# Cross-attention block with MLP: where GpSimd adds the MLP's output bias, and 28 warming matmuls

## The reference

```
q = layer_norm(x) @ q_w + q_b;  k = ctx @ k_w + k_b;  v = ctx @ v_w + v_b     # 16 heads of 32
p = softmax(q k^T / sqrt(32));  hidden = (p v) @ cproj_w + cproj_b + x
y = gelu(layer_norm(hidden) @ fc_w + fc_b)                                     # 512 -> 2048
out = hidden + (y @ proj_w + proj_b)                                           # 2048 -> 512
```

## Time and profile before

| | us |
|---|---|
| median of 3 runs | 719.77 |
| lowest, highest | 718.78, 721.11 |
| profiled execution, whole | 721.0 |
| its span, first to last instruction | 719.2 |

### The profile page before, as it was taken

How to read it: one execution, slowest core, us unless ns; L and a number is a source line. 1 busy time by engine, 2 the same in 40 slices (tenths; PEclk the granted TensorE clock), 3 DMA queues, 4 the chain that set the end, 5 groups by cost and what they waited for, 6 DMA issues and landing times.

```text
span 719.2 us, 13448 instructions
## 1 busy us (share of the span) xinstructions
PE 689.6 (96%) x4685; PEld 599.0 (83%) x4685; DVE 439.7 (61%) x867; ACT 313.8 (44%) x591; POOL 256.8 (36%) x228
## 2 busy tenths in 40 slices
PE   6889999999999999998899999999999999999998
PEld 5679898999998998897787888888888888888886
DVE  5689979979798888679865584423234322341122
ACT  4467867867676877578511023121111111111110
POOL 5285866657475758557503021011100111000000
PEclk9999999999999999999999999999999999999999
DMA  8895564637464644446109000100001000010001
GB/s 249 242 228 169 179 179 153 199 114 206 120 190 133 193 129 132 144 118 191 32 19 289 0 1 1 58 1 2 0 1 58 0 0 0 0 59 0 1 1 58
DMA packets 51153, 69.25 MB, mean 96 GB/s; under 512 B 8344, under 2 KB 29208, under 8 KB 51104
## 3 DMA queue, kind: packets, MB, share of 16 engines
q1 hardware_dynamic: 50832, 68.07, 32.3%
q0 software_dynamic: 272, 0.54, 0.4%
HBM read 47.21 MB, written 20.99 MB: 95 GB/s over the span
## 4 chain that ended last, share of the span: by engine, by line
PE 81%; DVE 5%; issue 4%; DMA 3%; ACT 3%; POOL 2%; SPq 2%; ACTq 0%; POOLq 0%; DVEq 0%
PE psum L1504 8%; PE psum L1503 8%; PE psum L1502 8%; PE psum L1487 8%; PE psum L1489 8%; PE psum L1488 8%; PE psum L1247 7%; PE psum L1249 7%; PE psum L1248 7%; PE psum L1293 4%; PE psum L1277 3%; PE psum L1398 2%; PE psum L1354 2%; POOL p_lo L562 2%; PE psum L1400 1%
## 5 line engine op out<-in xcount | busy, mean ns | idle before, releaser
L562 POOL TENSOR_TENSOR p_lo<-p,p_hi 128x512 f16<-128x512 f32 x128 | 157.1, 1231 | 94.2 <-ACT p_hi L682 93.6
L823 ACT ACTIVATE h<-psum,cols 128x512 f32<-128x512 f32 x64 | 44.1, 689 | 292.7 <-PE psum L1489 292.7
L1155 DVE CAST h_hi<-h 128x512 fp32r<-128x512 f32 x64 | 28.2, 441 | 207.3 <-ACT h L823 202.7
L1487 PE MATMUL psum<-y_hi,w_mlp 128*128 128x512 f32 x256 | 99.8, 390 | 1.4 <-DVE w_mlp L1116 1.4
L1502 PE MATMUL psum<-w_mlp,h_hi 128*128 128x512 f32 x256 | 100.8, 394 | 0.0
L1504 PE MATMUL psum<-w_mlp,h_lo 128*128 128x512 f32 x256 | 99.8, 390 | 0.0
L1503 PE MATMUL psum<-w_mlp,h_hi 128*128 128x512 f32 x256 | 99.7, 390 | 0.0
L1489 PE MATMUL psum<-y_hi,w_mlp 128*128 128x512 f32 x256 | 99.7, 389 | 0.0
L1488 PE MATMUL psum<-y_lo,w_mlp 128*128 128x512 f32 x256 | 99.6, 389 | 0.0
L680 ACT ACTIVATE p<-psum,maskbias 128x512 f32<-128x512 f32 x128 | 87.2, 682 | 21.9 <-PE psum L1277 20.1
L915 DVE TENSOR_REDUCE negm<-psum 128x2 f32<-128x512 f32 x128 | 83.7, 682 | 16.3 <-PE psum L1293 16.0
(11 more groups left out here) (111 smaller groups left out, 1493.6 us busy)
## 6 DMA issues: line engine op xcount, KB each, us to landing
qk_rows<-qk SPq DMA_DIRECT2D x32, 512.0 KB, 2.9
stacks<-qk_rows SPq DMA_DIRECT2D x64, 256.0 KB
stacks<-qk_rows SPq DMA_DIRECT2D x64, 128.0 KB
hidden<-in_x_dram SPq DMA_DIRECT2D x8, 512.0 KB, 4.1
ctx_sb<-in_ctx_dram SPq DMA_DIRECT2D x8, 512.0 KB, 4.7
w_mlp_raw<-in_L_xattn_fc_w_dram SPq DMA_DIRECT2D x16, 256.0 KB, 5.4
w_mlp_raw<-in_L_xattn_proj_w_dram SPq DMA_DIRECT2D x16, 256.0 KB, 6.1
out_dram<-hidden SPq DMA_DIRECT2D x16, 256.0 KB, 2.1
```

Source lines behind the costliest of these rows:

```text
L562: pool.tensor_tensor(p_lo[:, slot, :], p32[:, u % 2, :], p_hi[:, slot, :], ALU.subtract).then_inc(s["p_lo_done"], 1)
L1487: nc.tensor.matmul(bank, w[:, 0, :], y_hi[:, k, :], start=(k == 0), stop=False)
```

## The change

Three of the entries of WARM go (12, 5 and 11 matmuls), and pb(0) to pb(3) get one wait more each.

```diff
-        WARM = {("MX", 1, 0): 12, ("MX", 2, 0): 5, ("ST", 30, 0): 20, ("ST", 31, 0): 18, ("V", 31, 0): 20, 
-                ("attT", 0, 0): 11, ("begin", 0, 0): 36, ("mT", 0, 0): 19}
+        WARM = {("ST", 30, 0): 20, ("ST", 31, 0): 18, ("V", 31, 0): 20, 
+                ("begin", 0, 0): 36, ("mT", 0, 0): 19}
...
             def pb(j):
                 if isinstance(j, int) and j == 0:
                     pool.wait_ge(s["pb_loaded"], 16)
+                if isinstance(j, int) and j < CH:
+                    pool.wait_ge(s["h_lo_done"], j + 6)
                 pool.wait_ge(s["y_normed"], j + 1)
```

## The result

The changed kernel takes 724.38 us (median of 8 runs, 720.71 to 726.92), beside 719.90 for the kernel before in the same session; the ratio is 1.0051, 95% interval 1.0027 to 1.0076. It is slower by half a per cent, 5.5 us above the 718.9 that I predicted and outside the range. The profiled execution of the changed kernel took 726.92 us, with a span of 725.1 against 719.2.

A forecast was written before the change was run, and what follows sets the result against it. TensorE, busy 96% of the span, was taken as the bound. The terms -1.67 (old stall), +0.84 (new stall) and 0 (ones) summed to -0.83 us, from a median of 719.77 to 718.9 us; range 717.4 to 720.6.

The forecast's parts named there:

- Step 1: At fc(6): with the four adds gone, VectorE readies weights(6) earlier and TensorE's stall goes whole, gaining 1.67 us.
- the sum -1.67 + 0.84: Gain at fc(6) plus new stall at proj(9); with 0 for the ones, -0.83 us in all.
- Step 2: Adds behind split_h(5) to (8): the first three cost nothing, the fourth stalls TensorE at proj(9) by 0.84 us.
- D taken as 0.95: Delay in us of split_h(9)'s low part, as the fourth add slows VectorE's weights(9); bounds 0 and 1.42.
- The rival of the cheap add: Behind split_h(8): the fourth add costs little, stall 0 to 0.3 us, time 718.1 to 718.4; chance 0.16.
- Step 3: Removing the 28 ones at two scores groups and the first attention transpose: 0 us, bounds -1.57 and +1.7.
- The rival that the clock falls: Before group 2's scores at 45.5 us: longer gap drops the clock, up to 1.7 us lost, 720.6; chance 0.10.
- the sign I had named for being wrong: The granted clock dropping below 1.00 between 38 and 50 us, one of three such signs.
- Theory 1: From the experiments' expectations: the missing ones let TensorE's clock fall in their own gaps; f2 2 us or more slower.
- Theory 4: From the experiments: handover to MLP waits 1.0 (short) or 3.7 us (long rhythm) in either kernel; late ones force short.
- The gap at 287: Rival: TensorE's 2.04 us idle where the loop is left shortens, 1.7 us come back, 717.2; chance 0.09.
- The ones on the path: Rival: the 28 ones hold TensorE up after all, removal gives 1.57 us more, 717.4; chance 0.04.

The follow-up runs named there:

- g3: The kernel before, profiled again with no edit; profiled time 719.85 us.
- g1: The kernel before, profiled again with no edit; profiled time 726.09 us.
- e2: The kernel before without the 28 ones, the adds in their old place; 724.66 us, ratio 1.0041.
- f3: The kernel before plus 20 ones ahead of the scores of group 31, nothing else; 719.23 us, ratio 0.9971.
- e8: e1 with the fourth add one slice later, behind slice 9; 720.32 us, ratio 0.9977 to the kernel before.
- f1: Kernel before with adds behind slices 5, 6, 7, 9, all 28 ones kept, 20 ones added ahead of group 31's scores; 719.21 us, ratio 0.9979.
- f2: f1 without the 28 ones; 719.47 us, ratio 0.9991 to the kernel before.
- e3: The changed kernel with the 11 ones of the first attention transpose back; 723.03 us, ratio 1.0020 to the kernel before.
- e4: The changed kernel with the 12 and 5 ones of the scores back; 721.12 us, ratio 1.0014 to the kernel before.
- e7: The changed kernel plus 20 ones ahead of the scores of group 31; 721.09 us, ratio 0.9992 to the kernel before.
- e1: The kernel before with only the adds moved, behind slices 5 to 8, all ones in place; 720.34 us, ratio 0.9995.
- e5: The changed kernel with 28 more ones at the program's start; 723.11 us, ratio 1.0013 to the kernel before.

## Why the prediction was wrong, by its own steps

*Step 1, the adds leave their place: right in kind, its size holds for some executions only.* The three VectorE instructions came back to the durations given, and the stall at fc(6) went whole. But the stall is not one number. The waits of TensorE from 340 to 450 us in g3 and in g1, both the kernel before:

```profile
...
PE psum L1487 <- DVE w_mlp L1116: 0.7, 1, 0.7
```

```profile
...
PE psum L1487 <- DVE w_mlp L1116: 1.4, 1, 1.4
```

It is 1.4 in two profiles of the old place and 0.6 to 0.8 in three (g3, e2, f3). The first cast of split_h(3) makes the difference: beside the adds it took 1.36 and 1.41 us in the two, 0.57 to 0.72 in the three. With 1.4, E falls by 0.8 to 0.9, as the sum -1.67 + 0.84 had it. With the smaller stall it falls by 0.1 to 0.2: the new stall gives back nearly all that is gained.

*Step 2, the adds arrive: right.* The new stall is 0.85 us (0.84 predicted), at the place named, through the subtraction of weights(9), 0.97 longer (D taken as 0.95). Taken away in e8, f1 and f2 it gives back 0.9 us of E (363.7 to 363.8). The rival of the cheap add is out. It was half right in its mechanism, though: the cast at 412.54, which had begun when the add came, kept its 0.69 us, and the subtraction behind it paid. Of the pages cited, the Trainium skill's "GPSIMD Engine Reference", section Key points, is borne out (a VectorE instruction with two SBUF inputs suffers); "Advanced Engine Details and Errata", section VectorE Performance Modes, which names the 2-port ones alone, is not, by 2.20 us against 1.23.

*Step 3, the ones: this is the step that failed.* I took 0 for the three, because each group's end is not awaited; measured, their absence costs 2.5 us in the mean, and e2, which leaves out the ones alone, has the ratio 1.0041 [1.0008, 1.0074]. The reasoning looked at what a group delays and at the one gap behind it. It left out what the order of events behind the ones does to VectorE, GpSimd and the clock. In A that is a wait for cs of 2.6 us in place of 1.1, some 3 us behind the place of the eleven, in some executions, and more stretches at 1.2 GHz from 30 us on. In D it is the long rhythm, 260 us further on, though that the ones change its odds isn't shown. With 2.5 in place of 0 my sum would have been +1.7 us. In it an upper bound of +1.7 stood for the ones, with a chance of 0.10 for the rival that held it.

*The rival that the clock falls: its sign, its place in part, not its price.* It put the fall at 45.5 us. In the first profile of the changed kernel the clock falls at 33.4, 88.1, 292.9 and 350.9 us, and not between 38 and 50, which was the sign I had named for being wrong. In the six other profiles without the 28 it does fall there, and in three of the seven with them (g1, g3, e8). So Theory 1, that the clock falls in the ones' own gaps, may have a share in A, but it can't be the whole: it has no place for the rhythm, and f2 isn't slower than f1 by the 2 us that it asks for. Theory 4 is borne out in that either kernel takes either rhythm and that the late ones give the short one.

*The gap at 287* did not go with the change: in the first profile of the changed kernel the clock falls there as before. It is there by chance in either kernel, in before, g1, after and e2 and in no other profile, and it goes with a C of 58.2 us or more, where the others have 54.4 to 57.0. *The ones on the path* is out as far as can be told: removed, they gave nothing back, f2 against f1.

*The method had a flaw too.* I compared with one profile of before as if its waits were the kernel's. The kernel's executions run from 717 to 729 us, and a gap of 2.5 us between two profiles is inside that. My range of 3.2 us was narrower than this spread, and the terms I summed were as small as it.

**What stays open.** That the long rhythm is more frequent without the 28 (5 of 5 against 3 of 5) is not established by ten profiles, and how ones ahead of the loop could make a store late at 320 us is not shown. That the changed kernel is slower, and the one with late ones isn't, is measured. Which of the three groups matters is open: the times of e3 and e4 don't separate, though the wait of 2.6 us for cs came only without the eleven. And if A were 1.8 us longer without the 28 in every kind of kernel, f2 should be slower than f1 by that much; 0.3 was measured, and 1.8 lies at the edge of what those executions allow.

## What to carry to other kernels

A warming matmul can't be priced by the gap that it fills. Before removing one, look at the longest waits further on, and at what shortens them. Twenty ones ahead of the last scores did as much as the 28: with the adds behind slices 5 to 8, e7 (late ones alone) has the ratio 0.9992, e1 (the 28 alone) 0.9995, and the changed kernel, with neither, 1.0033 to 1.0051. By the profiles they did it by making TensorE later at a place where being early costs more, not by filling a gap in which the clock would fall. f1, the version that the experiments point to, has the median 719.21 us, ratio 0.9979 [0.9949, 1.0008], and f3, which needs no change to the adds, 719.23, 0.9971 [0.9938, 1.0003]: both clearly under the changed kernel (722.83 beside them), neither told apart from the kernel before. Profile a kernel several times before a stall of one microsecond in it is used as a term: here 1.4 was 0.7 in the next profile. And move an instruction that takes VectorE's time behind the low part that is awaited, not ahead of it: that was worth 0.9 us in E in all three profiles that have it, though no interval of the whole time shows it.

## What the runs showed of the hardware

The longer the wait, the surer the clock falls, but the wait alone doesn't decide. After a wait of 3.7 us for hidden there was a stretch at 1.2 GHz in all eleven profiles of the table that have it, of 3.4 or of 6.8 us; the second length costs 0.9 to 1.4 us more of D (21.8 to 21.9 against 22.8 to 23.2). After the wait of 1.0 us for hidden there was none in seven. The wait of 2.6 us for cs was followed by a stretch, at 87 to 91 us, in all four profiles that have it. The wait of 1.0 or 1.1 us for cs was followed by one in one profile of thirteen (e5, at 85.5). And between 30 and 55 us, where the first profile before has no wait over 1.3 us, the clock fell in ten of the first fourteen profiles and stayed up in four. The Trainium skill, "TensorE: Matmul & The Clock Gate", section What's actually happening, says that the activity monitor's window runs free and isn't reset by the kernel; the same 3.7 us of waiting with either length of stretch agrees with that, but no run here shows the window itself.

Both engines pay when VectorE's subtraction of 128x1024 runs beside GpSimd's add of 128x512: the subtraction takes 2.19 to 2.20 us instead of 1.23 when the add starts ahead of it, and the add 1.67 to 1.68 instead of 1.28.

A schedule written once can run in two fixed patterns. From the cast of weights(0) to the start of hidden it took 7.47 to 7.50 us in the seven profiles of the short rhythm and 8.93 to 9.08 in the eleven of the long one, with nothing between.
